# Bf16 spread with three exact parts, and right operands repeated to 112 and 120 columns, in the attention stage of a four-layer graph network

## The reference

```
h = (x @ W).reshape(n_nodes, H, C)
s_src = jnp.einsum('nhc,hc->nh', h, a_src)
s_dst = jnp.einsum('nhc,hc->nh', h, a_dst)
e = s_src[src] + s_dst[dst]
e = jnp.where(e > 0, e, NEG_SLOPE * e)
e_max = jax.ops.segment_max(e, dst, num_segments=n_nodes)
e_exp = jnp.exp(e - e_max[dst])
denom = jax.ops.segment_sum(e_exp, dst, num_segments=n_nodes)
alpha = e_exp / denom[dst]
msg = alpha[:, :, None] * h[src]
out = jax.ops.segment_sum(msg, dst, num_segments=n_nodes)
```

## Time and profile before

| what | value |
|---|---|
| median of 3 runs | 10230.54 us (10212.95 to 10238.89) |
| the profiled execution | 10236.32 us, span 10234.6 us |
| granted TensorE clock, mean | 0.753 of 2.4 GHz |
| first to last weigh of round 1 | 5159 to 6693 us |
| first to last weigh of round 2 | 6784 to 8301 us |

### The profile page before, as it was taken

One profiled execution on the slowest core, in us unless ns is written; L12 is line 12 of the kernel. 1 busy time (PEld: TensorE's weight loads), 2 busy tenths in 40 slices (PEclk: granted clock), 3 DMA queues, 4 the chain that ended last, 5 costly groups with the idle time before them and its releaser, 6 DMA issues. The chain is left out here.

```text
span 10234.6 us, 159905 instructions
## 1 busy us (share of the span) xinstructions
PE 7980.2 (78%) x42704; PEld 5943.4 (58%) x42743; DVE 4696.9 (46%) x12866; ACT 1497.5 (15%) x2199; POOL 3633.0 (35%) x3461
## 2 busy tenths in 40 slices
PE   0466206666666569999889999989999969995999
PEld 0355103333432235555589999979999955553555
DVE  7777615555554422222256666656666650103011
ACT  2122001111111110100022222212222210000000
POOL 0777775555532000000065555545556510000000
PEclk9877657777766679999955555556556569997999
DMA  0222002222212146777521111111111126663666
GB/s 14 61 71 69 17 14 73 74 74 73 72 64 55 49 124 173 189 180 178 139 53 38 38 37 38 36 40 39 38 37 39 38 65 189 190 191 88 191 192 182
DMA packets 871568, 901.04 MB, mean 88 GB/s; under 512 B 421539, under 2 KB 820226, under 8 KB 864867
## 3 DMA queue, kind: packets, MB, share of 16 engines
q1 hardware_dynamic: 753541, 637.16, 22.6%
q0 software_dynamic: 109664, 179.92, 7.8%
q10 hardware_dynamic: 8064, 80.29, 1.9%
HBM read 722.84 MB, written 93.87 MB: 80 GB/s over the span
## 5 line engine op out<-in xcount | busy, mean ns | idle before, releaser
L1886 POOL DMA_INDIRECT d_row_ring<-table_att,src_at x1664 | 1766.6, 1062 | 1369.4 <-SPq L1843 802.1
L776 PE MATMUL psum<-b_hot 128*128 x2860 | 885.9, 454 | 1075.5 <-DVE b_hot L948 1018.4
L2380 PE MATMUL psum<-e_a_ring,e_parts 128*128 128x448 bf16 x8232 | 1579.1, 353 | 83.1 <-DVE e_parts L2462 75.9
L2380 PEld LDWEIGHTS psum<-e_a_ring,e_parts 128*128 128x128 bf16 x8232 | 806.7, 98 | 824.8 <-issue 89.0
L776 PEld LDWEIGHTS psum<-b_hot 128*128 x2860 | 315.6, 110 | 1590.6 <-issue 1463.9
L759 POOL DMA_INDIRECT b_row_ring<-edge_attr,b_entry x896 | 884.8, 987 | 975.4 <-SPq L737 735.3
L1926 PE MATMUL psum<-edges_out,edges_in 128*128 128x132 f32 x4896 | 1171.7, 433 | 22.8 <-DVE edges_out L2123 22.0
L1926 PEld LDWEIGHTS psum<-edges_out,edges_in 128*128 128x128 f32 x4896 | 1098.0, 333 | 28.2 <-DVE edges_out L2123 27.5
L351 POOL DMA_INDIRECT listed<-a_record,a_slot_no x832 | 927.8, 1115 | 341.9 <-issue 273.4
L1911 PE MATMUL psum<-edges_out,edges_in 128*128 128x28 f32 x4896 | 954.3, 359 | 59.1 <-ACT edges_in L1972 33.7
L1911 PEld LDWEIGHTS psum<-edges_out,edges_in 128*128 128x128 f32 x4896 | 934.8, 292 | 82.7 <-issue 58.0
(11 more groups left out here) (414 smaller groups left out, 7899.6 us busy)
## 6 DMA issues: line engine op xcount, KB each, us to landing
e_a_ring<-adjacency SPq DMA_DIRECT2D x1372, 224.0 KB, 2.8
c_a_ring<-adjacency SPq DMA_DIRECT2D x686, 224.0 KB, 2.9
adjacency<-b_line ACTq DMA_DIRECT2D x49, 1568.0 KB
a_cum<-edge_attr SPq DMA_DIRECT2D x103, 512.0 KB
d_row_ring<-table_att,src_at POOLq DMA_INDIRECT x1664
b_row_ring<-edge_attr,b_entry POOLq DMA_INDIRECT x896
listed<-a_record,a_slot_no POOLq DMA_INDIRECT x832
e_a_left<-adjacency_left SPq DMA_DIRECT2D x28, 224.0 KB, 3.2
```

The costliest lines, as they stand in the source:

```text
L776: mm = nc.tensor.matmul(ps[:, v, :], hot[:, at, j, 0:P].rearrange("p a f -> p (a f)"), hot[:, at, j, P + v * WIN:P + (v + 1) * WIN].rearra ...
L1886: pool.indirect_dma_start(out=row_ring[:, u % 4, g, :], out_offset=None, in_=table_att[layer], in_offset=bass.IndirectOffsetOnAxis(ap=src_ ...
L2380: mm = nc.tensor.matmul(psum[:, 2 * (turn % 2) + v, 0:WIN], parts[:, piece, s, :], a_ring[:, s % SEVEN, v * WIN:(v + 1) * WIN], start=(s = ...
```

## The change

Spread goes from f32 to bf16. Every f32 value that is spread is cut into three bf16 parts whose sum is the value, so `to_edge` has 24 columns in place of 8. `from_dst` is bf16. The parts of the node's own values are made once per round for all tiles (`to_parts`). Those of the peaks are made in `peak`, with more small instructions on DVE. The node's f32 peaks stand in `peaks` now. `shift` begins with a `tensor_reduce` that adds the three parts of each value. The semaphore `s_me`, for which spread waits, is raised behind the last part.

The right operands of rank and spread are read several times over by a stride of zero: 28 columns four times (112), 24 columns five times (120). What lands beyond a chunk's own columns is overwritten by the next chunk's product, or stands behind the last one and is not read.

`is_dst_b` and `turned` now lie in the space that the narrower `from_dst` leaves. The diff, cut to its core:

```
-            is_dst, from_dst = (flat_in[:, k * 3 * G * P:(k + 1) * 3 * G * P].rearrange("p (u g f) -> p u g f", u=3, g=G)
-                                for k in range(2))
+            is_dst = flat_in[:, 0:3 * G * P].rearrange("p (u g f) -> p u g f", u=3, g=G)
+            from_dst = flat_in[:, 3 * G * P:3 * G * P * 3 // 2].bitcast(BF16).rearrange("p (u g f) -> p u g f", u=3, g=G)
...
-                        mm = nc.tensor.matmul(ps_slots[h][:, c, :], is_dst[:, h, c, :], ranked[:, h, c, :],
-                                              start=True, stop=True)
+                        mm = nc.tensor.matmul(psum[:, 2 + h, c * WITH:(c + AGAIN) * WITH], is_dst[:, h, c, :],
+                                              bc(ranked[:, h, c, :], 1, [P, AGAIN, WITH]), start=True, stop=True)
...
-                        mm = nc.tensor.matmul(ps_spread[:, c, :, :].rearrange("p w f -> p (w f)"), from_dst[:, h, c, :],
-                                              to_edge[:, h, :, :].rearrange("p w f -> p (w f)"), start=True, stop=True)
+                        mm = nc.tensor.matmul(psum[:, 6, c * SPREAD:(c + AGAIN_SPREAD) * SPREAD], from_dst[:, h, c, :],
+                                              bc(to_edge[:, h, :, :, :].rearrange("p w f k -> p (w f k)"), 1, [P, AGAIN_SPREAD, SPREAD]),
+                                              start=True, stop=True)
...
-                    V.tensor_tensor(to_edge[:, h, 1, :], logit[:], now, ALU.max).then_inc(s_me, 1)
-                    dve.wait_ge(s_me, at + 1)
-                    B.by(V.tensor_tensor(drop[:, h, :], now, to_edge[:, h, 1, :], ALU.subtract))
+                    B.by(V.tensor_tensor(peaks[:], logit[:], now, ALU.max))
+                    B.settle(dve)
+                    B.by(V.tensor_copy(to_edge[:, h, 1, :, 0], peaks[:]))
+                    B.by(V.tensor_tensor(drop[:, h, :], now, peaks[:], ALU.subtract))
                     B.settle(dve)
                     dve.sem_inc(s_drop, 1)
-                    B.by(V.tensor_copy(now, to_edge[:, h, 1, :]))
+                    B.by(V.tensor_tensor(peak_rest[:], peaks[:], to_edge[:, h, 1, :, 0], ALU.subtract))
+                    B.by(V.tensor_copy(now, peaks[:]))
+                    B.settle(dve)
+                    B.by(V.tensor_copy(to_edge[:, h, 1, :, 1], peak_rest[:]))
+                    B.settle(dve)
+                    V.tensor_tensor(to_edge[:, h, 1, :, 2], peak_rest[:], to_edge[:, h, 1, :, 1], ALU.subtract).then_inc(s_me, 1)
...
-                    C.by(V.tensor_tensor(raw[:], rows_at(code[1])[:, :, FEAT:], ps_spread[:, :, 0, :], ALU.add))
+                    C.by(V.tensor_reduce(spread_sum[:].rearrange("p g w f -> p (g w f)"),
+                                         ps_spread.rearrange("p g (w k) -> p (g w) k", k=3), AX_X, ALU.add))
+                    C.settle(dve)
+                    C.by(V.tensor_tensor(raw[:], rows_at(code[1])[:, :, FEAT:], spread_sum[:, :, 0, :], ALU.add))
```

More of the change, by code:

```diff
@@ L1718, in gnn_kernel @@
             WITH = SLOTS + HEADS
+            AGAIN = P // WITH
+            SPREAD = 2 * HEADS * 3
+            AGAIN_SPREAD = P // SPREAD
             in_pairs = sbb("in_pairs", [P, P * QI], I32)
@@ L1739, in gnn_kernel @@
             flat_out = edges_out[:].rearrange("p t f -> p (t f)")
-            is_dst, from_dst = (flat_in[:, k * 3 * G * P:(k + 1) * 3 * G * P].rearrange("p (u g f) -> p u g f", u=3, g=G)
-                                for k in range(2))
+            is_dst = flat_in[:, 0:3 * G * P].rearrange("p (u g f) -> p u g f", u=3, g=G)
+            from_dst = flat_in[:, 3 * G * P:3 * G * P * 3 // 2].bitcast(BF16).rearrange("p (u g f) -> p u g f", u=3, g=G)
             weighted = flat_out[:, 0:G * FEAT].rearrange("p (g f) -> p g f", g=G)
             ranked = flat_out[:, G * FEAT:G * (FEAT + 3 * WITH)].rearrange("p (u g f) -> p u g f", u=3, g=G)
-            is_dst_b = sbb("is_dst_b", [P, 3, G, P], BF16)
+            is_dst_b = flat_in[:, 3 * G * P * 3 // 2:6 * G * P].bitcast(BF16).rearrange("p (u g f) -> p u g f", u=3, g=G)
             key_near = sbb("key_near", [P, G], I16)
@@ L1750, in gnn_kernel @@
             logit = sbb("logit", [P, HEADS])
-            to_edge = sbb("to_edge", [P, 3, 2, HEADS])
+            to_parts = sbb("to_parts", [P, NT + 1, HEADS, 3], BF16)
+            to_rest = sbb("to_rest", [P, NT + 1, HEADS])
+            to_edge = sbb("to_edge", [P, 3, 2, HEADS, 3], BF16)
+            peaks = sbb("peaks", [P, HEADS])
+            peak_rest = sbb("peak_rest", [P, HEADS])
+            spread_sum = sbb("spread_sum", [P, G, 2, HEADS])
             drop = sbb("drop", [P, 3, HEADS])
@@ L1760, in gnn_kernel @@
             y = [sbb(f"y{i}", [P, 4, D]) for i in range(2)]
-            turned = [is_dst_b[:, i, :, :].bitcast(F32).rearrange("p g f -> p (g f)").rearrange("p (j f) -> p j f", f=P)
+            turned = [flat_in[:, G * P * (9 + i) // 2:G * P * (10 + i) // 2].rearrange("p (j f) -> p j f", f=P)
                       for i in range(2)]
@@ L1810, in gnn_kernel @@
             ps_slots = [psum[:, 2 + h, 0:G * WITH].rearrange("p (g s) -> p g s", g=G) for h in range(3)]
-            ps_spread = psum[:, 6, 0:G * 2 * HEADS].rearrange("p (g w f) -> p g w f", g=G, w=2)
+            ps_spread = psum[:, 6, 0:G * 2 * HEADS * 3].rearrange("p (g k) -> p g k", g=G)
             ps_out = psum[:, 7, 0:FEAT]
@@ L2044, in _ @@
                 n_pass, last = passes_of(dve)
-                A, B, C, E_ = Stage(s_A, 2), Stage(s_B, 8), Stage(s_C, 3), Stage(s_E, 1)
+                A, B, C, E_ = Stage(s_A, 2), Stage(s_B, 12), Stage(s_C, 4), Stage(s_E, 1)
                 def rows_at(batch):
@@ L2076, in peak @@
                     mine = to_logit[:, one, :].rearrange("p a f -> p (a f)")
+                    mine_parts = to_parts[:, one, :, :].rearrange("p a f k -> p (a f) k")
                     dve.wait_ge(s_slots, at + 1)
@@ L2080, in peak @@
                                          ps_slots[h][:, :, SLOTS:SLOTS + 1].broadcast_to([P, G, RANKS + 1]), ALU.is_ge))
-                    B.by(V.tensor_copy(to_edge[:, h, 0, :], mine))
+                    B.by(V.tensor_copy(to_edge[:, h, 0, :, :], mine_parts))
                     B.settle(dve, 1)
@@ L2106, in shift @@
                     C.settle(dve)
-                    C.by(V.tensor_tensor(raw[:], raw[:], ps_spread[:, :, 1, :], ALU.subtract))
+                    C.by(V.tensor_tensor(raw[:], raw[:], spread_sum[:, :, 1, :], ALU.subtract))
                     C.settle(dve)
@@ L2166, in _ @@
                     st4.by(V.tensor_tensor(all_logit[:], every, to_logit[:, 0:NT, :], ALU.add))
+                    st4.by(V.tensor_copy(to_parts[:, :, :, 0], to_logit[:]))
+                    st4.settle(dve)
+                    st4.by(V.tensor_tensor(to_rest[:], to_logit[:], to_parts[:, :, :, 0], ALU.subtract))
+                    st4.settle(dve)
+                    st4.by(V.tensor_copy(to_parts[:, :, :, 1], to_rest[:]))
+                    st4.settle(dve)
+                    st4.by(V.tensor_tensor(to_parts[:, :, :, 2], to_rest[:], to_parts[:, :, :, 1], ALU.subtract))
                     st4.settle(dve)
```

## The result

The changed kernel takes **9955.15 us** (median of 4 runs, 9941.36 to 9994.65) against 10223.14 us. The ratio is 0.9743, with a 95% interval of 0.9712 to 0.9774: 268 us less, where 375 were forecast. The profiled execution has a span of 9992.1 us and a mean clock of 0.829. With 9994.65 us it is the longest of the four (the others took 9941 to 9957), so a body in the profile takes some 0.13 us more than in the median run (39.5 us over 306 bodies, an estimate).

What follows compares the result with a forecast made beforehand. PE was taken to bound at 10.04 us per body. DVE would bind next at 8.6, plus 0.2 for low-clock bodies and late rows: 8.8, so 376 us off 10236 gives 9860 profiled, 9855 for runs; range 9730 to 10100.

Steps and rivals of the forecast that it cites:

- the case to which I gave 0.66: Attention loops: DVE becomes the bound at 8.6 to 9.1 us per body, 9800 to 9950 us; chance 0.66.
- the case of the rows: Rival on POOL: DVE's denser work slows row DMAs by a fifth, 9.1 to 9.3 us per body, 9950 to 10010; chance 0.05.
- rank's times: Sign on PE: rank's sixteen pairs no longer than 3.5 us at 1.2 GHz and near 1.8 at 2.4.
- the waits for L2114 and of `is_dst_b`: Signs: PE waits for L2114 ahead of spread; L2066 (`is_dst_b`) hardly waits for PE, against 2.1 to 2.3 us before.
- The bound moves away from PE: Attention loops: the bound goes from PE at 10.04 us per body to DVE at 8.6.
- The loop through DVE and ACT: PE's chain of gather, L2066, ACT's widening and rank: 9.80 us per body at 1.2 GHz, 6.5 at 2.4.
- The clock rises with the width: PE in the loops: with wide rank and spread the clock is mostly high, between 0.7 and 0.9.
- The rival that the clock stays low: PE idles in real gaps and its clock stays low: 9.3 to 9.8 us per body, 10010 to 10163; chance 0.14.
- The columns are free: Rank on PE: going from 28 to 112 columns costs 0.05 us, bounded by nothing and 0.29 at 1.2 GHz.
- The weight load follows the clock: PE's f32 pairs with full load shorten at 2.4 GHz: 0.99 us for eight in place of 1.86, ratio 0.53.
- DVE at 8.6 per body: DVE's pace: 7.43 us plus 1.18 for extra instructions in `peak`, address step and `shift`; bounds 8.3 to 8.9.
- Rows: the term that was mis-sized: POOL's row fetch: 10.7 us per unit, 7.3 per body, below DVE's 8.6; its 802 us wait for slots shrinks.

Runs made afterwards that it cites:

- with rows free: Changed kernel with SP's word for a free ring slot moved ahead of the wait for the previous unit's landing: 9810.24 us, ratio 0.9591.
- SP's step: SP's free-slot word moved ahead of the previous unit's landing: 9810.24 us in the changed kernel, 9468.52 in the kernel before with repeated operands, 10233.18 in it alone.

## Why the prediction was right, and where its size was off

The time fell into the range, and PE lost the lead, as forecast. But the sum named DVE as the next bound, and in the changed kernel it was the fetch of the rows. Some of this was luck: the case to which I gave 0.66, DVE's at 9800 to 9950, ended 5 us below the measured time and was not what happened; the range held the result because it also held the case of the rows, to which I gave 0.05. Of the signs in the forecast the loops (1345 us each), DVE's share (over 80%), rank's times and POOL's wait (below 400 us) failed; PE's share, the clock, spread's time and the waits for L2114 and of `is_dst_b` came as said.

- **The bound moves away from PE: right.** PE's busy share fell to 69%, DVE's wait for it ahead of `is_dst_b` from 483 us (1.58 per body) to 34. The loop through DVE and ACT showed in the kernel without repetition: 9.47 us per body at a clock of 0.58, against the 9.80 forecast for the lower clock alone.
- **The clock rises with the width: right, and shown.** 0.58 with 28 and 24 columns, 0.84 with 112 and 120 in the same bf16 kernel, and 0.87 by the repetition alone. The rival that the clock stays low falls: PE was idle for 31% of the loops, in gaps of 0.3 to 1.3 us in the body shown, and the clock was 0.84 all the same. At 0.84 the clock's share left little on the path: with rows free a body takes 8.64.
- **The columns are free: nearly right for f32, not for bf16.** At the lower level sixteen rank pairs took 3.56 us with 28 columns and 3.73 with 112, which is 0.17 where 0.05 was taken and 0.29 was the bound. At the higher level they took 1.94 (28 columns, in the kernel with only spread repeated) and 2.01. "If rank grows" was a sign of being wrong, and it grew a little. Spread's eight bf16 pairs took 0.35 us with 24 columns and 0.59 with 120 at the higher level. That costs no time here, since PE waits anyway.
- **The weight load follows the clock: right.** Sixteen rank pairs took 2.01 us at the higher level and 3.73 at the lower, sixteen gather pairs 2.07 and 3.89. The Trainium skill's formula for the load (TensorE: Matmul & The Clock Gate, section "LDWEIGHTS (loading the stationary operand)") leaves the clock out. The traces disagree with it, by these pairs and by the 1.86 and 0.99 us of the earlier trace rows.
- **DVE at 8.6 per body: right as its own pace, wrong as the bound of the changed kernel.** Without late rows the body is 8.64. The extra instructions were put at 1.18 us. The fair measure is the pair of kernels with wide operands and SP's step, with and without the bf16 parts: 9810 against 9469, 342 us or 1.12 per body. The second of these is bound by POOL, so the parts themselves may cost slightly more.
- **Rows: the term that was mis-sized.** The step reads: "One unit of rows costs 8 x 1.062 us and its share of the issue gaps [...] It now waits 802 us for free slots, and that wait shrinks." I took all 802 us for slack. At 200 units POOL waits at least 2.64 us, mostly about 2.75, some 550 us in all, for the landing of the unit before. This part doesn't shrink, and it is nearly all of the 563.5 us that are left after the change. So POOL's pace was not 7.3 us per body but 9.26 (1.84 of waiting and 0.14 of longer DMAs on top), above DVE's 8.6. The trace of before held this: none of the 200 gaps was below 2.64 us. A body of the profiled execution missed the forecast by 9.25 - 8.8 = 0.45 us: DVE's waits for rows are 0.63, and the 0.2 that I had allowed for them and for low stretches comes off. Taking the landing away gave 145 us (9955 to 9810), which is below the 9855 that I had forecast for the change alone. The rival "rows come late" had the right place and the right price (9.1 to 9.3 us, 9950 to 10010), but the wrong mechanism: the DMAs were not a fifth slower (1086 ns against 1062).
- **Where the gain comes from.** The short spread alone brings 165 us, the repetition on top of it some 90 (by the ratios) to 106 (by the medians) more, and the rows cap it there. With the rows free the repetition is worth 250 (10061 to 9810). The bf16 spread then costs more than it brings: without it, with both operands repeated all the same, the kernel is 342 us faster.

## What to carry to other kernels

In this kernel an f32 product with a full weight load and few columns left room for more columns: 84 more cost 0.17 us of 3.56. They raised the granted clock, and that was worth more than a cheaper product. Before an engine's wait is taken for slack, look at single gaps of it: a gap with the same floor every time is a latency in the chain, and it becomes the bound as soon as the engine that hid it gets faster. A queue that hands out free slots should not stand behind the landing of what was issued before.

## What the runs showed of the hardware

- The clock did not answer to thin products in proportion to their share. In the f32 kernels widening only one of two thin products (from 8 to 120, or from 28 to 112 columns) brought it from 0.58 to 0.95 or 0.91, and 56 columns in both brought 0.90. In the bf16 kernels spread alone brought 0.69 and rank alone 0.87.
- A body of wide f32 products ran at a clock of 0.99 while PE's loops held it busy 85% of the time. The thin ones at 98% busy had 0.58. The busy share of the page did not tell the clock.
- At the lower level sixteen f32 pairs took 3.56 us with 28 columns and 3.73 with 112, at the higher 1.94 and 2.01. Eight bf16 pairs took 0.35 us with 24 columns and 0.59 with 120 at the higher level: there the columns were not hidden.
- From the end of a unit's last row DMA on POOL to the next unit's first, through the landing and SP's word, took at least 2.64 us in the kernel before, in the changed one and in the one with only the repeated operands. The medians of the last two are 2.77 and 2.76 us.
